# A two-layer attention and expert kernel: first beginning and row scale reordered, second attention's mask moved into the score product

## The reference, cut to what matters

```
# layer 0: attention of normed x over ctx (ctx is key and value), then a mixture of 16 experts
scores = hs @ ctx.T / 16 ; scores = where(keep, scores, -1e30)
x = x + where(any(keep), softmax(scores) @ ctx, 0)
x = x + moe0(norm(x)) + shared0(norm(x))
# layer 1: 16 heads of 16 features; k = ctx @ Wk.T + bk, v = ctx @ Wv.T + bv
s = q @ k.T / 4 ; s = s + where(mask > 0, 0, -1e30)
p = clip(exp(s), e^-50, e^50) ; o = (p @ v) / (sum(p) * (1 + 1e-8))
x = x + norm(rs * (o @ Wo.T + bo)) ; x = x + moe1(norm(x)) + shared1(norm(x))
```

## Time and profile before

| | |
|---|---|
| median of 3 runs | 760.24 us (758.79 to 761.08) |
| profiled execution | 762.05 us, of which the span of the trace is 759.1 us |
| PE busy | 695.1 us, 92% |
| DVE busy | 544.3 us, 72% |
| ACT busy | 397.7 us, 52% |
| DMA | 131.14 MB, mean 173 GB/s |

### The profile page before, as it was taken

The page is one execution under the profiler, slowest core; times in us unless marked ns, Lnnn a source line. Parts: engine busy times, 40 slices in busy tenths (PEclk is TensorE's granted clock), DMA queues, the critical chain, the costliest instruction groups (busy, mean ns, idle before and its releaser), DMA issues.

```text
span 759.1 us, 14907 instructions
## 1 busy us (share of the span) xinstructions
PE 695.1 (92%) x5499; PEld 538.5 (71%) x5499; DVE 544.3 (72%) x1174; ACT 397.7 (52%) x564; POOL 173.8 (23%) x220
## 2 busy tenths in 40 slices
PE   3798999989889999999999699999999999998990
PEld 3798999988678888888888554454454454677880
DVE  6767576777486666666666788789888878766655
ACT  2643333334322322222222699999999999533550
POOL 5462524340000000000000050002303604442551
PEclk9899999999999999999999899999999999799996
DMA  7456484832627777677768959986969740464545
GB/s 247 133 172 227 134 293 146 266 125 89 201 65 242 231 255 239 209 224 243 253 217 170 149 81 168 189 128 95 221 92 201 119 67 2 151 253 130 165 129 190
DMA packets 55211, 131.14 MB, mean 173 GB/s; under 512 B 10112, under 2 KB 36096, under 8 KB 51568
## 3 DMA queue, kind: packets, MB, share of 16 engines
q1 hardware_dynamic: 51888, 122.93, 60.8%
q0 software_dynamic: 2256, 6.18, 2.4%
q10 hardware_dynamic: 1008, 1.25, 0.5%
HBM read 78.78 MB, written 48.79 MB: 168 GB/s over the span
## 4 chain that ended last, share of the span: by engine, by line
PE 64%; issue 11%; ACT 11%; DVE 10%; DMA 3%; SPq 1%; POOL 0%; DVEq 0%; POOLq 0%; ACTq 0%
PE ps L657 15%; PE ps L658 14%; PE ps L659 14%; ACT p L1439 8%; PE ps L1001 5%; PE ps L1189 4%; PE ps L959 3%; PE ps L1205 2%; PE ps L1023 1%; PE ps L741 1%; DVE valid L1571 1%; DVE rscale L1626 1%; PE ps L1173 1%; DMA raw<-in_ctxT 1%; ACT hh L1344 1%
## 5 line engine op out<-in xcount | busy, mean ns | idle before, releaser
L1439 ACT ACTIVATE p<-ps,kbias 128x1024 f32<-128x1024 f32 (+1 forms) x208 | 211.4, 1163 | 5.1 <-PE ps L959 4.9
L1950 DVE TENSOR_SCALAR p<-p 128x1024 f32<-128x1024 f32 (+1 forms) x208 | 140.8, 689 | 25.8 <-ACT p L1439 24.1
L1001 PE MATMUL ps<-p,vsl 128*17 128x256 f32 (+1 forms) x1664 | 114.2, 383 | 2.0 <-DVE p L1950 1.0
L959 PEld LDWEIGHTS ps<-qst,kst 48*128 48x128 f32 (+1 forms) x832 | 58.6, 182 | 60.0 <-ACT p L1439 32.1
L1344 ACT ACTIVATE hh<-h 128x512 fp32r<-128x512 f32 x50 | 31.6, 632 | 132.2 <-DVE h L1817 115.2
L959 PE MATMUL ps<-qst,kst 48*128 48x256 f32 (+1 forms) x832 | 91.1, 318 | 5.3 <-ACT p L1439 1.5
L360 POOL TENSOR_SCALAR nv<-mv 128x2 f32<-128x2 f32 x8 | 6.2, 777 | 358.8 <-DVE mv L1880 211.2
L657 PE MATMUL ps<-xTh,w_hi 128*128 128x512 f32 x200 | 79.8, 399 | 1.5 <-DVE h L1813 0.8
L658 PE MATMUL ps<-xTl,w_hi 128*128 128x512 f32 x200 | 79.2, 396 | 0.0
L659 PE MATMUL ps<-xTh,w_lo 128*128 128x512 f32 x200 | 78.9, 394 | 0.0
L1001 PEld LDWEIGHTS ps<-p,vsl 128*17 128x17 f32 (+1 forms) x1664 | 35.7, 96 | 40.0 <-DVE p L1950 7.2
(11 more groups left out here) (308 smaller groups left out, 1558.8 us busy)
## 6 DMA issues: line engine op xcount, KB each, us to landing
x_slots<-blank SPq DMA_DIRECT2D x20, 1032.0 KB, 5.9
kst<-k_hi SPq DMA_DIRECT2D x64, 200.2 KB, 8.4
w_raw<-in_w SPq DMA_DIRECT2D x25, 384.0 KB, 3.5
v_one<-vst SPq DMA_DIRECT2D x4, 1768.0 KB, 9.9
vsl<-v_one SPq DMA_DIRECT2D x4, 1768.0 KB, 17.0
kst<-k_lo SPq DMA_DIRECT2D x32, 200.2 KB, 8.5
raw<-in_ctxN SPq DMA_DIRECT2D x12, 512.0 KB, 5.6
e_w<-in_w SPq DMA_DIRECT2D x2, 3072.0 KB, 15.3
```

The costliest lines, as they stand in the source:

```text
L959: mm = pe.matmul(ps[0:rows, 2 * (x % RING) + t, c * SEQ:(c + 1) * SEQ], kst[r, job % KSL, c, m * P:m * P + rows], qst[r, b, 2 * g + c, :], ...
L1001: mm = pe.matmul(ps[32 * j:32 * j + VW, 6 + job % 2, 0:SEQ], vsl[0:rows, b % 2, at_:at_ + VW], p32[0:rows, x % PBUF, (2 * t + c) * SEQ:(2 ...
L1439: act.activation(p32[0:rows, x % PBUF, :], psf[0:rows, bank * 512:bank * 512 + 1024], ACT.Exp, scale=0.25, bias=kbias[0:rows, col:col + 1] ...
L1950: dve.tensor_scalar(t, t, CLO, CHI, ALU.max, ALU.min).then_inc(p_clip, 1)
```

## The change

In the first attention `any_key` and `row_scale` move behind the second value evacuation of the tile; `row_scale` becomes a `tensor_scalar`. In the first tile of all, the third key projection goes ahead of `trans(0, 0)`, the square root of the later rows moves behind `pth(0, 1)`, two dummy activations load ACT's tables early, the high and low parts come in another order, and the normed rows of tiles 4 to 7 are made behind `norm_lo(1)`.

In the second attention the per-partition operand `kbias` goes. Each head gets a 17th row in the key memory that holds -2^100 for a masked key and 0 otherwise (computed by DVE, stored by SP in round 3 of the first experts); the third load of a half takes 17 rows instead of 16, the stack has 49 rows, and the 49th row of the queries is one.

```diff
-KR = 3 * HD
+KR = 3 * HD + 1
+BAR = -2.0 ** 100
...
-    kh_d = nc.dram_tensor("k_hi", [NB * D, MP], F32).ap()
+    kh_d = nc.dram_tensor("k_hi", [NB * NH * (HD + 1), MP], F32).ap()
...
+                    if r == 3:
+                        sp.wait_ge(bar_rdy, 1)
+                        for b in range(NB):
+                            sp.dma_start(kh_d.rearrange("(b h r) n -> b r h n", b=NB, r=HD + 1)[b, HD:HD + 1, :, :], bar_f[b:b + 1, :].unsqueeze(1).broadcast_to([1, NH, MP])).then_inc(row_out, 16)
...
-                for t, dr in ((kh, kh_d), (kl, kl_d)):
-                    sp.dma_start(dr[b * D + mt * P:b * D + mt * P + P, c0:c0 + w], t[:, slot, 0:w].bitcast(F32)).then_inc(k_out[slot], 16)
+                u = b * NH + mt * (P // HD)
+                head_rows = kh_d.rearrange("(u r) n -> u r n", r=HD + 1)[u:u + P // HD, 0:HD, c0:c0 + w]
+                sp.dma_start(head_rows, kh[:, slot, 0:w].bitcast(F32)).then_inc(k_out[slot], 16)
+                sp.dma_start(kl_d[b * D + mt * P:b * D + mt * P + P, c0:c0 + w], kl[:, slot, 0:w].bitcast(F32)).then_inc(k_out[slot], 16)
...
+                hi = kh_d.rearrange("(j c t r) n -> j r c t n", c=2, t=2, r=HD + 1)[job]
+                lo = kl_d[rows, :].rearrange("(c t r) n -> r c t n", c=2, t=2)
                 for t in range(2):
-                    for part, dr in enumerate((kh_d, kl_d, kh_d)):
+                    for part, (dr, n) in enumerate(((hi, HD), (lo, HD), (hi, HD + 1))):
                         at_ = 64 * t + HD * part
-                        sp.dma_start(kst[at_:at_ + HD, job % KSL, :, :].bitcast(F32),
-                                     dr[rows, :].rearrange("(c t r) n -> r c t n", c=2, t=2)[:, :, t, :]).then_inc(k_in[job % KSL], 16)
+                        sp.dma_start(kst[at_:at_ + n, job % KSL, :, :].bitcast(F32), dr[0:n, :, t, :]).then_inc(k_in[job % KSL], 16)
...
+            def ones_rows(lo, hi, done):
+                for t in range(2):
+                    row = slice(64 * t + KR - 1, 64 * t + KR)
+                    every = qst[row, :, :, :].rearrange("o b h (i n) -> o (b h i) n", n=P)
+                    sp.dma_start(every[:, lo:hi, :].bitcast(F32), ones[0:1, :].bitcast(F32).unsqueeze(1).broadcast_to([1, hi - lo, P])).then_inc(done, 16)
...
+            queries(0, 1)
+            ones_rows(4, per, q_in[1])
+            queries(0, 2)
...
                 if i:
                     readout(i - 1)
+                else:
+                    kproj(b, h + 2)
                 trans(i, 0)
...
             act.wait_ge(cst_set, 2)
+            act.activation(warm[:, 0:1], eps[:], ACT.Sqrt)
...
+            first_hi(0)
             norm_hi(0)
+            first_hi(1)
+            act.activation(warm[:, 1:2], eps[:], ACT.Exp)
...
                 act.activation(p32[0:rows, x % PBUF, :], psf[0:rows, bank * 512:bank * 512 + 1024], ACT.Exp,
-                               scale=0.25, bias=kbias[0:rows, col:col + 1]).then_inc(p_exp, 1)
+                               scale=0.25).then_inc(p_exp, 1)
...
-                dve.tensor_tensor(rscale[:], rsum[:], valid[:], ALU.mult).then_inc(rscale_rdy, 1)
+                dve.tensor_scalar(rscale[:], rsum[:], valid[:, 0:1], None, ALU.mult).then_inc(rscale_rdy, 1)
...
-                if h == 0:
-                    any_key(b)
-                row_scale(i)
...
                 vev(b, h)
                 ptl(i, 3)
-                for n in range(h + 1, h + 4):
+                vev(b, h + 1)
+                if h == 0:
+                    any_key(b)
+                row_scale(i)
+                for n in range(h + 2, h + 4):
                     vev(b, n)
                 if h == 0 and b + 1 < NB:
                     norm_lo(b + 1)
+                if i == 0:
+                    norm_rows(4, NT, 1)
...
-                dve.wait_ge(cw_in, 16 * 8)
+                dve.wait_ge(cw_in, 16 * 9)
+                dve.tensor_scalar(bar_f, bar_i, 0.5, BAR, ALU.is_le, ALU.mult).then_inc(bar_rdy, 1)
```

More of the change, by code:

```diff
@@ L155, in build @@
             g_beats4 = Bt("g_beats4", [P, NT, 4 * 5])
-            Bt("gap3b", [P, 2032])
+            bar_w = Bt("bar_w", [P, MP], I32)
+            bar_i, bar_f = bar_w[0:NB, :], bar_w[0:NB, :].bitcast(F32)
+            Bt("gap3b", [P, 2032 - MP])
             g_rank = Bt("g_rank", [P, NT, E])
@@ L523, in queries @@
                 restack(half, g, 2)
-            for g in range(1, NG - 1):
-                queries(0, g)
+            def ones_rows(lo, hi, done):
[3 more added lines that the diff above has]
+                    sp.dma_start(every[:, lo:hi, :].bitcast(F32), ones[0:1, :].bitcast(F32).unsqueeze(1).broadcast_to([1, hi - lo, P])).then_inc(done, 16)
+            per = NH // 2 * SEQ // P
+            sp.wait_ge(tri_rdy, 1)
+            queries(0, 1)
+            ones_rows(4, per, q_in[1])
+            queries(0, 2)
             for job in range(KSL, NJ):
@@ L531, in _ @@
                     queries(0, NG - 1)
+                    ones_rows(per + 4, 2 * per, q_in[NG - 1])
                 if job == KSL + 1:
                     values(1)
+                if job == 2 * KSL:
+                    ones_rows(2 * per, NB * per, q_in[NG])
                 for g in {2 * KSL: (0,), 2 * KSL + 1: (1, 2), 2 * KSL + 2: (3,)}.get(job, ()):
@@ L707, in scores @@
                     for k in range(KT):
+                        if x == 0 and k == 1:
+                            pe.wait_ge(ctx_split, raw_t(0, 1) + 1)
                         mm = mm3(pe, ps[:, SB0 + x % 2, 0:w], xTh[:, k, s], xTl[:, k, s],
@@ L763, in _ @@
                     readout(i - 1)
+                else:
+                    kproj(b, h + 2)
                 trans(i, 0)
-                kproj(b, h + 2)
+                if i:
+                    kproj(b, h + 2)
                 trans(i, 1)
@@ L1240, in _, with first_hi @@
             act.wait_ge(cst_set, 2)
+            act.activation(warm[:, 0:1], eps[:], ACT.Sqrt)
             act.wait_ge(ln_mv, 2)
             act.activation(std[:, 0:2], mv[:, 0:2, 1], ACT.Sqrt, bias=eps[:]).then_inc(ln_std, 1)
-            for k in range(2):
+            def first_hi(k):
                 act.wait_ge(raw_in[k], 16)
@@ L1311, in _ @@
                 pth(i, 1)
+                if i == 0:
+                    act.wait_ge(ln_mv, NT)
+                    act.activation(std[:, 2:NT], mv[:, 2:NT, 1], ACT.Sqrt, bias=eps[:]).then_inc(ln_std, 1)
                 kev(b, h + 3)
@@ L1433, in _ @@
                 job, m = at(x)
-                rows, col = rows_of(m), job // NG * MT + m
+                rows = rows_of(m)
                 act.wait_ge(sc_rdy, x + 1)
@@ L1548, in norm_front, with norm_rstd @@
                     dve.bn_aggr(mv[:, t, :], st6[:, t, :]).then_inc(ln_mv, 1)
-            def norm_rows(t0, t1, n):
+            def norm_rstd(t0, t1, n):
                 dve.wait_ge(ln_std, n + 1)
@@ L1553, in norm_rows @@
                 dve.wait_ge(ln_rstd, n + 1)
+            def norm_rows(t0, t1, n):
                 for t in range(t0, t1):
@@ L1656, in _ @@
                 dve.tensor_tensor(cTl[:, 0, k, 0:1024], raw[:, k, :], cTh[:, 0, k, 0:1024].bitcast(F32), ALU.subtract).then_inc(ctx_split, 1)
-            norm_lo(0)
+                if k == 0:
+                    norm_lo(0)
             masks(0)
@@ L1688, in _ @@
                 if i == 0:
-                    norm_rows(2, NT, 1)
-                    dve.wait_ge(keep_in, 16)
-                    dve.tensor_scalar(kbias[:], keep[:], 0.5, -1e30, ALU.is_le, ALU.mult).then_inc(kbias_rdy, 1)
+                    norm_rstd(2, NT, 1)
+                    norm_rows(2, 4, 1)
                     dve.wait_ge(vstk_set, 2)
@@ L1970, in delta @@
             def delta(t, n, o):
+                if t == 0:
+                    dve.wait_ge(d_w, 8)
                 dve.wait_ge(dl_rdy, t + n)
@@ L2317 @@
         "attend": np.pad(get("mask_BxS2_bk0").view(np.uint8), ((0, 0), (0, 4 * MW - M))).view(np.int32),
-        "keep": np.pad(get("mask_BxS2_ik0"), ((0, 0), (0, MT * P - M))).reshape(NB * MT, P).T,
+        "keep": np.pad(get("mask_BxS2_ik0"), ((0, 0), (0, MP - M))),
         "wqT": tr("L1_xattn_Wq"), "wkT": tr("L1_xattn_Wk"), "wvT": tr("L1_xattn_Wv"), "woT": tr("L1_xattn_Wo"),
         "bq": get("L1_xattn_bq").reshape(KT, P).T,
-        "bq0": np.tile(get("L1_xattn_bq")[0:HG * HD].reshape(2, 2, 1, HD), (1, 1, 64 // HD, 1)).reshape(2, P).T, "bk": get("L1_xattn_bk").reshape(KT, P).T, "bv": get("L1_xattn_bv"), "bo": get("L1_xattn_bo"),
+        "bq0": np.concatenate([np.tile(get("L1_xattn_bq")[0:HG * HD].reshape(2, 2, 1, HD), (1, 1, 3, 1)), np.ones((2, 2, 1, HD), np.float32)], axis=2).reshape(2, P).T, "bk": get("L1_xattn_bk").reshape(KT, P).T, "bv": get("L1_xattn_bv"), "bo": get("L1_xattn_bo"),
         "gam": get("L1_xattn_ln_gamma"), "bet": get("L1_xattn_ln_beta"), "rs": get("L1_xattn_residual_scale").reshape(1),
```

31 lines of the change are left out of this document (15 added, 16 removed).

## The result

The changed kernel takes 954.8 us (median of 4 runs, 952.4 to 955.7) against 760.7 us before: a ratio of 1.254, 95% interval 1.251 to 1.258. I had forecast 883 us with a range of 800 to 955: the sign and the mechanism came out, the size did not (+194 instead of +123). That 954.8 lies inside the range, by 0.2 us, is luck: the range of the one-engine case itself ended at 945. The profiled execution has a span of 950.1 us.

A forecast was written before the change was run, and what follows sets the result against it. It took PE as the bound in the first attention and experts, ACT in the second attention. Without key loads 760.2 - 5.5 - 13.5 = 741 us; with 17 rows on one engine 760.2 + 123 = 883 us, range 800 to 955.

The forecast's parts named there:

- the one-engine case: Second attention: all 17 rows of a load go to one DMA engine; 883 us, own range 820 to 945, chance 0.78.
- Key loads: Second attention: 17-row loads cost 0 if dealt unevenly, or 21 us a job on one engine, above 12.4 otherwise needed.
- 336 + 17 + 12 = 365 us from 396: Second attention, busiest engine: 16 jobs by 21 us, values 17, restacks about 12, starting at 396 us; last keys at 761.
- my share for the four other loads: Second attention: the busiest engine's sixteenth of a job's other four key loads, 51 KB, adds 1.9 to 6.3 us.
- the middle case: Second attention: the halves' 17-row loads fall on two different engines, 14 us a job; 740 to 790, say 765; chance 0.05.
- 16.3 less 3: Second attention: exponential's gain summed over jobs, less 3 us for level engines and two extra `ones_rows` transfers; given as 13.5.
- Exponential: Second attention: dropping the per-partition operand shortens 1165 ns to about 1074; gain 13.5 us, bounds 8 and 18.9.
- so it is next: Second attention: PE becomes the next bound after ACT's exponential shortens, PE 197 us against ACT 196.
- First attention: First attention: the 9.1 us of stalls go, a later wait stays; gain 5.5 us, bounds 2 and 9.
- less 0.5 for a longer store of the high keys: First attention: 0.5 us taken off the gain of 6 for longer high-key stores ahead of the context loads.
- Between: cost 0: Between the attentions: mask rows computed while DVE idles, four row stores beside PE-bound experts; cost 0, without cover some 2 us.
- The table loads: First tile: the 1.28 us table load leaves the exponential's path; a drain would add 1.4 us, but the trace shows none.

The follow-up runs named there:

- row17: Kernel before, with only the third key load of a half bringing 17 rows instead of 16 (last job excepted): 936.5 us, 1.233.
- row18: Kernel before, with only the third key load of a half bringing 18 rows instead of 16: 764.8 us, 1.006.
- halforder: Against the kernel before plus 17-row third loads in the first half only (841.1 us): query restacks issued ahead of key loads: 837.3 us.
- exponly: Kernel before, with only the second attention's exponential losing its per-partition operand, key mask left out: 754.5 us, 0.991.
- spread: As split, but the four stores of mask rows are issued one in each of four expert rounds: 755.0 us, 0.991.
- split: Changed kernel, with 16-row key loads again and the mask rows of both halves in one transfer of their own: 767.1 us, 1.0075.
- first: Kernel before with the first attention's part of the change alone, keys stored as before: 755.7 us, 0.991.
- best: Changed kernel with high keys in plain rows, mask rows in their own tensor by one store, one mask-row transfer per job, 16-row loads: 747.5 us, 0.982.
- halfpool: Kernel before, with 17-row third key loads in the first half only, these issued by GpSimd instead of SP: 857.6 us, 1.126.

## Why the prediction was half right

**Key loads: right in kind, too small.** Seventeen rows go to one engine (share 0.06, one packet at a time), keys bound the stage, ACT is busy 51% of it: as I had it. My stated reason was a judgement; the runs confirm it. The rule of the Trainium skill, "DMA: Bandwidth & Descriptors", section "Why a DMA increments its semaphore by 16 and not by 1", says so, and by it 18 rows go to nine; row17 and row18, 937 and 765 us with one and nine packets at once, agree with both. The step that fell short is the sum over that engine. I added up 336 + 17 + 12 = 365 us from 396; it is 407 from 415.6. In it a job has 16.8 + 6.3 = 23.1 us: the upper end of my share for the four other loads, where I had taken 21, some 33 us over sixteen jobs; values and restacks are 38 instead of 29. And the start: 20 us later, which goes through to the end undiminished, since the engine hardly ever runs dry. 20 for the start and 42 for the sum are 62 of the 71 us between +123 and +194; the rest lies between the account's end at 823 and the last exponential. Two slips of my sums changed nothing here: by my own terms a job turns slower at 13.3 us on the busiest engine, (651.4 - 13.5 - 29 - 396) / 16, not at 13.9, so that the middle case would be 771 rather than 765, and 16.3 less 3 is 13.3.

**Shape of the loss.** I had all jobs 18 to 24 us from the fourth on. Job 0 took 52.5 us, because SP is held in the issue of 17-row loads and the queries for job 1 stand behind it; job 7 38 us, in which DVE waits 22.4 us for the last restacks; jobs 4, 8 and 12 hold the values' loads, whose landing went from 17.0 to 34.7 us. By halforder this is where the time shows, not what it is.

**Exponential.** 1165 to 1040 ns in the changed kernel and 1054 to 1056 where keys are in time, predicted 1074; a step from 1.00 to 0.90 us (9 exponentials in a row take 8.29 us in exponly). In the changed kernel it is worth nothing, since keys are awaited. With keys in time it is worth 6 to 7 us, not 13.5. The step that failed is PE's sum in "so it is next", and with it the 3 us taken off for the two being level: I had PE at 197 and ACT at 196 us for the stage. Over spread's whole stage of 216.3 us ACT is busy 199.4, near my sum, but PE 209.9 (195.1 of the 200.4 without the first job). And around queries and output products each waits for the other in turn, ACT 0.6 to 2.8 us, PE 0.4 to 1.8 (jobs 7, 11 and 15 are longer than before). The stage fell by 5.9 us in split and 6.1 in spread, below my lower bound of 8; exponly as a whole gave 6.9 (4.3 to 9.7).

**First attention.** The 9.1 us stall went, and the wait I named as next late, `sS` behind `norm_lo`, came: predicted. The size failed: +5.5 predicted, -2.7 measured. The step is "less 0.5 for a longer store of the high keys". The stores take 0.57 us to issue instead of 0.32 to 0.45 and the loads behind them 1.5 us longer to the cast; that moves the stall behind the loads, where it stands in one piece and brings the lower clock behind all three waits, where I had it only vanish. `norm_rows(4, 8)` ahead of `row_max(1)`, 2.5 us where I had 1.5 and priced it at 0, is on the path in sample 0. By the rule of the Trainium skill named above, stores of 128 rows against 8 heads use eight engines, which would double an engine's share of such a store. The packets agree: in the changed kernel the stores of two key units (512 packets) run for long with 8 in flight and take 4.8 to 5.8 us, before with 16 and 2.4 to 3.2 us. Which part of the 9 us between this kernel and `first` is the engines and which the longer issue was not parted.

**Between: cost 0.** Wrong, 9 us of stall and some 12 with the clock. The computation of the rows was hidden, as I had it; I had waved the four stores through as lying "beside the PE-bound experts", without asking what they read. One partition of 6408 bytes, read sixteen times, keeps all engines busy: a packet takes 3.4 us, while in `best` four packets of the same size from four partitions take 0.25 to 0.46. Those go to other target rows too, so that the shared partition is the cause is likely but not parted from the target.

**The table loads.** The first exponential starts 0.08 us behind `nmax` instead of 1.37: the load's 1.28 us left the path and nothing more, so the trace shows no drain beside it.

## What to carry to other kernels

Before a row is added to a transfer, factor its row count: here 16 rows went to sixteen engines, 18 to nine and 17 to one, and what counts is then that engine's work summed over the stage, all other transfers' shares included, from the first issue to the last. Give an odd row a transfer of its own. Let the loads that the next wait hangs on go ahead of stores in the same queue, and ask of each store not only how many bytes it has but from how many partitions it reads.

## What the runs showed of the hardware beyond that

- The queue that issues is held when one engine's work piles up: two issues took 12.4 us instead of 0.8 (425.7 to 438.1), for the last 4 us of it with the share at 0.06, fifteen engines idle.
- The row scale has one column per partition: with two tensor operands in the memory beside the engines it took 159 to 2004 ns before, the same work with its second operand as a scalar per partition 212 to 216 ns (lines L1626 of before and L1658 of after):

```profile
L1626 DVE TENSOR_TENSOR rscale<-rsum,valid x8: 159/1046/2004, 27.1 to 176.7; 128x1 f32<-128x1 f32 x8
```

```profile
L1658 DVE TENSOR_SCALAR rscale<-rsum,valid x8: 212/214/216, 33.5 to 187.7; 128x1 f32<-128x1 f32 x8
```

The 2004 ns are at 70.33, while GpSimd's split runs (69.94 to 74.66); the 159 ns at 176.72, where GpSimd is idle; the six others, 614 ns and more, all meet GpSimd at work. In the changed kernel none of the eight meets it, since the row scale has moved, so that kernel can't tell form from place; `first` can: two of its eight run inside a GpSimd split (97.40 and 138.19) and take 214 and 216 ns. The Trainium skill, "SBUF — State Buffer", section "Who interferes with whom", says that a VectorE instruction with two inputs there contends with GpSimd's reads, and one with at most one input, outside the two-port modes, does not; these rows agree with both.
- In `halfpool` GpSimd's own queue cut rows of 6408 bytes into packets of some 410 bytes: a load of 212.8 KB took 17.8 us.
